# Last turns of a transformer kernel: low halves on VectorE, a pipelined softmax list, the last output product in one piece

## The reference

```
h = tokens(x)                                   # an S4D kernel, made once for all batches
h = h + attention(layernorm(h))                 # 32 query heads, 8 key heads, head size 32, causal, rotary
h = h + layernorm(h) @ W.T + b + sum_e alpha_e * lora_e(layernorm(h))   # 4 active experts of rank 8, alpha by a router
```

## Time and profile before

| what | us |
|---|---|
| median of 3 runs (2893.61 to 2898.27) | 2895.41 |
| the profiled execution: device time | 2895.14 |
| its span, first to last instruction | 2893.2 |
| TensorE busy | 2799.6 (97%) |
| VectorE busy | 2366.2 (82%) |
| ScalarE busy | 1918.2 (66%) |
| GpSimd busy | 1970.2 (68%) |
| mean granted TensorE clock, share of full | 0.991 |
| the ending, from TensorE's first scores of Z to the end of the span | 2811.05 to 2893.2 |

### The profile page before, as it was taken

How to read it: one execution, slowest core, us unless ns; L and a number is a source line. 1 busy time by engine, 2 the same in 40 slices (tenths; PEclk the granted TensorE clock), 3 DMA queues, 4 the chain that set the end, 5 groups by cost and what they waited for, 6 DMA issues and landing times.

```text
span 2893.2 us, 61884 instructions
## 1 busy us (share of the span) xinstructions
PE 2799.6 (97%) x16932; PEld 1408.5 (49%) x16932; DVE 2366.2 (82%) x8776; ACT 1918.2 (66%) x5986; POOL 1970.2 (68%) x1730
## 2 busy tenths in 40 slices
PE   6788899999999999999999999999999999999997
PEld 5665444444444444444444444444444444444443
DVE  9987788888888888888888888888888888888784
ACT  8887766666666666666666666666666666666662
POOL 4542677777777776777777777777767777777763
PEclk9999899999999999999999999999999999999999
DMA  7884677666666666666666666666666666666763
GB/s 246 231 217 135 142 153 150 149 149 151 151 143 152 146 156 147 151 149 147 152 148 149 149 150 151 143 152 147 156 149 148 150 146 152 150 149 149 152 132 78
DMA packets 1220851, 442.64 MB, mean 153 GB/s; under 512 B 1167120, under 2 KB 1175568, under 8 KB 1220640
## 3 DMA queue, kind: packets, MB, share of 16 engines
q1 hardware_dynamic: 1220640, 440.69, 66.7%
HBM read 88.22 MB, written 67.11 MB: 54 GB/s over the span
## 4 chain that ended last, share of the span: by engine, by line
PE 89%; DVE 3%; DMA 3%; ACT 2%; issue 1%; POOL 1%; SPq 1%; DVEq 0%; ACTq 0%; POOLq 0%
PE bank_b L2068 44%; PE bank_a L2068 22%; PE bank_c L2068 11%; PE score L2031 4%; PE kps L581 2%; PE pv L2057 2%; DMA tok_h<-kout 2%; PE bank_b L2057 1%; PE bank_b L2227 1%; DMA xc<-in_x_dram 1%; PE pv L2160 1%; ACT kout L358 1%; ACT probs L1440 0%; PE bank_c L2121 0%; PE pv L2121 0%
## 5 line engine op out<-in xcount | busy, mean ns | idle before, releaser
L1440 ACT ACTIVATE probs<-probs,negmax 128x128 f32<-128x128 f32 x2016 | 777.3, 387 | 247.4 <-DVE negmax L1658 247.3
L1303 POOL TENSOR_TENSOR p_hl<-probs,p_hl 128x512 f16<-128x512 f32 x503 | 607.6, 1208 | 333.9 <-ACT p_hl L1449 331.4
L1299 POOL TENSOR_TENSOR probs<-probs,rsum 128x512 f32<-128x512 f32 x503 | 547.6, 1089 | 183.5 <-DVE rsum L1669 183.1
L1658 DVE CUSTOM_DVE_ANT_0 probs<-score,table,scal 128x128 f32<-128x128 f32 x2016 | 589.0, 347 | 78.1 <-issue 77.4
L2068 PE MATMUL bank_a<-qkv_hi,xt 128*128 128x512 f16 x2048 | 642.6, 380 | 2.0 <-DMA xt<-xy_hl 2.0
L2068 PE MATMUL bank_b<-b_hi,yt 128*128 128x512 f16 x1952 | 610.7, 379 | 0.0
L1449 ACT ACTIVATE p_hl<-probs 128x512 f16<-128x512 f32 x503 | 314.5, 625 | 417.8 <-POOL probs L1299 417.8
L1712 DVE TENSOR_TENSOR heads<-rope_a,heads 128x512 f16<-128x512 f32 x319 | 388.1, 1232 | 30.0 <-ACT heads L1470 29.9
L2068 PE MATMUL bank_a<-qkv_lo,xt 128*128 128x512 f16 x1024 | 389.7, 381 | 0.0
L1440 ACT ACTIVATION_READ_ACCUMULATOR probs<-probs,negmax 128x1 f32 x2016 | 376.5, 187 | 0.0
L2068 PE MATMUL bank_b<-o_hi,at_hi 128*128 128x512 f16 x992 | 376.4, 379 | 0.0
(11 more groups left out here) (311 smaller groups left out, 4590.2 us busy)
## 6 DMA issues: line engine op xcount, KB each, us to landing
hin<-tok_h SPq DMA_DIRECT2D x64, 512.0 KB, 3.2
r<-tok_h SPq DMA_DIRECT2D x64, 512.0 KB, 3.8
out_dram<-r SPq DMA_DIRECT2D x63, 512.0 KB, 3.0
tok_h<-kout SPq DMA_DIRECT2D x60, 512.0 KB, 6.1
probs_t<-p_hl SPq DMA_TRANSPOSE x512, 3.1
xc<-in_x_dram SPq DMA_DIRECT2D x32, 128.0 KB, 4.5
raw_a<-in_L_attn_wq_dram SPq DMA_DIRECT2D x4, 1024.0 KB, 9.2
raw_b<-in_L_attn_wo_dram SPq DMA_DIRECT2D x8, 512.0 KB, 4.8
```

What stands on the lines that cost most here:

```text
L1299: TT(x, x, rsum[:, u % 4].unsqueeze(2).to_broadcast([P, GR, T]), ALU.mult).then_inc(s_norm, 1)
L1303: TT(p_hl[:, u % 2, 1], probs[:, u % 4], p_hl[:, u % 2, 0], ALU.subtract).then_inc(s_plo, 1)
L1440: ins = A(probs[:, u % 4, g], probs[:, u % 4, g], ACT.Exp, bias=negmax[:, u % 4, g:g + 1], scale=-1.0, accum_out=sums[:, u % 4, g:g + 1])
L1658: ins = V.tensor_tensor_reduce(probs[:, u % 4, g], score[u % 2][:, g], mask, col(U_SC), 3e38, ALU.add, ALU.min, negmax[:, u % 4, g:g + 1])
```

## The change

- GpSimd: the subtractions `low(X)` and `low(Y)` are gone, the bias additions of X and Y move behind all groups, `shift_of(X)` moves ahead of group 0 and `shift_of(Y)` between groups 6 and 7. The groups are pipelined: normalisation u, then the low half of u-1.
- VectorE: two new functions make whole rows and low rows for X, Y and Z. The list is reordered: X's second addition and statistics come first; the whole and low rows of Y stand around `routes(X)` and ahead of `weigh(X)`.
- ScalarE: `norm2` writes only the high half. `norm2(X)` moves up, `router_exp(X)` behind `probs_high(Z, 5)` but still ahead of `exps(7)`, `turned_z(X)` behind `probs_high(Z, 7)`.
- SyncE: the transpose of X's rows moves between groups 0 and 1, the last transpose of heads behind it.
- TensorE: `scores(7)` ahead of `ffn(X, 0)`; `attend(Z, 1)` ahead of `wo(Z)`; the four quarters of `wo(Z)` in a row, and `route(Y)` and `ffn(Y)` behind them.

```diff
@@ SyncE @@
                 residual(Y)
+                turn_probs(Z, 0)
+                turn_rows(X)
                 sp.wait_ge(s_hlo, Z * 5 + MADE[3])
                 sp.wait_ge(s_score, Z * 8)
                 sp.dma_start_transpose(stack[:, 3], heads[:, BLOCK[3]].rearrange("p h t -> p (h t)")).then_inc(s_st[3], 16)
-                turn_probs(Z, 0)
-                turn_probs(Z, 1)
-                turn_rows(X)
-                for u in range(2, 8):
+                for u in range(1, 8):
                     turn_probs(Z, u)
@@ GpSimd @@
                 def add_bias(c):
                     pool.wait_ge(s_yhi, c + 1)
-                    if c == Z:
-                        pool.wait_ge(s_ylo, c + 1)
+                    pool.wait_ge(s_ylo, c + 1)
...
                 normalise(Y, 7)
                 probs_low(Y, 7)
+                shift_of(X)
                 normalise(Z, 0)
+                for u in range(1, 7):
+                    normalise(Z, u)
+                    probs_low(Z, u - 1)
+                shift_of(Y)
+                normalise(Z, 7)
+                probs_low(Z, 6)
+                probs_low(Z, 7)
                 add_bias(X)
                 add_bias(Y)
@@ ScalarE @@
-                    ins = A(xy_hl[:, 0], r[:, c % 2], ACT.Identity, bias=shift2[:, 0:1], scale=rstd2[:, 0:1])
-                    if c != Z:
-                        ins = A(xyn[:, :], r[:, c % 2], ACT.Identity, bias=shift2[:, 0:1], scale=rstd2[:, 0:1])
-                    ins.then_inc(s_yhi, 1)
+                    A(xy_hl[:, 0], r[:, c % 2], ACT.Identity, bias=shift2[:, 0:1], scale=rstd2[:, 0:1]).then_inc(s_yhi, 1)
...
                 exps(0)
+                norm2(X)
                 exps(1)
...
                 exps(6)
+                probs_high(Z, 5)
                 router_exp(X)
-                probs_high(Z, 5)
                 exps(7)
                 probs_high(Z, 6)
-                turned_z(X)
                 norm2(Y)
                 probs_high(Z, 7)
+                turned_z(X)
@@ VectorE @@
+                def whole_rows(c):
+                    dve.wait_ge(s_rstd2, c * 2 + 2)
+                    if c == X:
+                        dve.wait_ge(s_xlo, CB)
+                    TS(xyn[:, :], r[:, c % 2], rstd2[:, 0:1], shift2[:, 0:1], ALU.mult, ALU.add).then_inc(s_xyn, 1)
+
+                def low_rows(c):
+                    dve.wait_ge(s_xyn, c - X + 1)
+                    dve.wait_ge(s_yhi, c + 1)
+                    TT(xy_hl[:, 1], xyn[:, :], xy_hl[:, 0], ALU.subtract).then_inc(s_ylo, 1)
...
                 invert(Y, 7)
+                add_wo(X, 1)
+                spread(X)
                 maxima(0)
                 attention_low(Y, 0)
                 maxima(1)
+                whole_rows(X)
                 invert(Z, 0)
+                maxima(2)
+                low_rows(X)
+                invert(Z, 1)
...
                 spread(Y)
-                routes(X)
                 maxima(7)
                 invert(Z, 6)
+                whole_rows(Y)
+                routes(X)
+                invert(Z, 7)
+                low_rows(Y)
                 weigh(X)
                 add_ffn(X, 0)
-                invert(Z, 7)
+                add_ffn(X, 1)
                 attention_low(Z, 0)
-                add_ffn(X, 1)
+                attention_low(Z, 1)
                 add_lora(X, 0)
                 add_lora(X, 1)
...
@@ TensorE @@
                 scores(6)
                 route(X)
-                ffn(X, 0, 0, 4)
                 scores(7)
-                ffn(X, 0, 4, 8)
+                ffn(X, 0, 0, 8)
                 ffn(X, 1, 0, 4)
                 turn_z(X)
                 ffn(X, 1, 4, 8)
                 pe.wait_ge(s_max, Z * 8 + 7)
                 attend(Z, 0)
                 lora(X)
+                pe.wait_ge(s_max, Z * 8 + 8)
+                attend(Z, 1)
                 wo(Z, 0, 0, 4)
                 wo(Z, 1, 0, 4)
-                pe.wait_ge(s_max, Z * 8 + 8)
-                attend(Z, 1)
-                route(Y)
-                ffn(Y, 0, 0, 3)
                 wo(Z, 0, 4, 8)
                 wo(Z, 1, 4, 8)
-                ffn(Y, 0, 3, 8)
+                route(Y)
+                ffn(Y, 0, 0, 8)
                 ffn(Y, 1, 0, 4)
                 turn_z(Y)
                 ffn(Y, 1, 4, 8)
```

More of the change, by code:

```diff
@@ L1382, in shift_of @@
                     TT(shift2[:, :], mean2[:, :], rstd2[:, :], ALU.mult).then_inc(s_rstd2, 1)
-                def low(c):
-                    pool.wait_ge(s_yhi, c + 1)
-                    TT(xy_hl[:, 1], xyn[:, :], xy_hl[:, 0], ALU.subtract).then_inc(s_ylo, 1)
                 def add_bias(c):
                     pool.wait_ge(s_yhi, c + 1)
-                    if c == Z:
-                        pool.wait_ge(s_ylo, c + 1)
+                    pool.wait_ge(s_ylo, c + 1)
                     TT(r[:, c % 2], r[:, c % 2], keep["bias"][:, :], ALU.add).then_inc(s_bias, 1)
@@ L1395, in ending @@
                 probs_low(Y, 7)
+                shift_of(X)
                 normalise(Z, 0)
-                probs_low(Z, 0)
-                normalise(Z, 1)
-                probs_low(Z, 1)
-                shift_of(X)
-                normalise(Z, 2)
-                low(X)
-                probs_low(Z, 2)
-                normalise(Z, 3)
-                probs_low(Z, 3)
-                add_bias(X)
-                normalise(Z, 4)
-                probs_low(Z, 4)
-                normalise(Z, 5)
-                probs_low(Z, 5)
-                shift_of(Y)
-                normalise(Z, 6)
-                probs_low(Z, 6)
-                normalise(Z, 7)
-                probs_low(Z, 7)
-                low(Y)
+                for u in range(1, 7):
[5 more added lines that the diff above has]
+                probs_low(Z, 7)
+                add_bias(X)
                 add_bias(Y)
@@ L1604, in ending @@
                 probs_high(Z, 1)
-                norm2(X)
                 attention_high(Y, 1)
@@ L1952, in ending @@
                    rope_a[:, 8:16].unsqueeze(2).to_broadcast([P, 8, 2, HD]), hi, ALU.subtract).then_inc(s_hlo, 1)
-                maxima(2)
-                invert(Z, 1)
-                add_wo(X, 1)
-                spread(X)
                 maxima(3)
+                attention_low(Y, 1)
                 invert(Z, 2)
-                attention_low(Y, 1)
                 maxima(4)
@@ L1968, in ending @@
                 spread(Y)
-                routes(X)
                 maxima(7)
                 invert(Z, 6)
+                whole_rows(Y)
+                routes(X)
+                invert(Z, 7)
+                low_rows(Y)
                 weigh(X)
                 add_ffn(X, 0)
-                invert(Z, 7)
+                add_ffn(X, 1)
                 attention_low(Z, 0)
-                add_ffn(X, 1)
+                attention_low(Z, 1)
                 add_lora(X, 0)
                 add_lora(X, 1)
-                attention_low(Z, 1)
-                routes(Y)
                 add_wo(Z, 0)
@@ L1983, in ending @@
                 spread(Z)
+                routes(Y)
+                whole_rows(Z)
                 weigh(Y)
-                dve.wait_ge(s_rstd2, Z * 2 + 2)
-                dve.wait_ge(s_ylo, Z)
-                TS(xyn[:, :], r[:, Z % 2], rstd2[:, 0:1], shift2[:, 0:1], ALU.mult, ALU.add).then_inc(s_xyn, 1)
-                dve.wait_ge(s_xyn, 1)
-                dve.wait_ge(s_yhi, Z + 1)
-                dve.wait_ge(s_yt, Z * 16)
-                TT(xy_hl[:, 1], xyn[:, :], xy_hl[:, 0], ALU.subtract).then_inc(s_ylo, 1)
+                low_rows(Z)
                 add_ffn(Y, 0)
```

## The result

| what | before | after |
|---|---|---|
| median of 7 runs, us | 2895.05 (2892.99 to 2898.27) | 2903.68 (2902.59 to 2907.06) |
| ratio, with its 95% interval | | 1.0033 (1.0024 to 1.0043) |
| the profiled execution: device time, us | 2895.14 | 2902.59 |
| its span | 2893.2 | 2900.6 |
| TensorE's first scores of Z, to the end of the span | 2811.05, 82.15 us | 2810.66, 89.94 us |

The kernel became slower by 0.33%, or 8.6 us between the medians. The forecast was 2900.6 us with a range up to 2904.5, so the time lies inside; but I had given "within 0.2%" the largest chance (0.50), and it is slower by more than that. Everything ahead of the ending is the same code, and the profile puts the loss where the forecast had put it, into the ending, 7.8 us.

A forecast was written before the change was run, and what follows sets the result against it. Batch Z's softmax chain, for which TensorE waits, was taken to bound the ending. turn_z(X) at 2851.9 plus 7.35 gave W = 2859.25; plus 39.2, a span of 2898.45; plus 2.2, 2900.6 us. Range 2893.5 to 2904.5.

The forecast's parts named there:

- within 0.2%: Whole kernel: time not told from no change, 2889.6 to 2901.2 us; chance 0.50, against slower 0.40 and faster 0.10.
- the queue: Rival, SyncE: rows of X and heads delay group 1's transpose, landing 2 us later at 2831.8; 2902.6 us, chance 0.24.
- W: Ending, first product of wo(Z,0) on TensorE: 2849.07 before, forecast 2859.25, ten us later, with 39.2 us to the end.
- part 3: Softmax list of batch Z: weigh(X) comes late, two bias additions add 2 x 2.2 us, turn_z(X) at 2851.9.
- e7: Start of the exponentials of group 7 on ScalarE: forecast 2840.7, before 2841.03; GpSimd's last low half ends 6.4 us later.
- the landing of group 1: SyncE's transpose of group 1: issued 2826.8, landed 2829.8; ScalarE's high half of group 3 needs that buffer.
- the base: Kernel before, last part of the ending: 25.9 us to ffn(Y,1)'s last product, then 18.2 us to the end.
- Part 1: Last output product in one piece on TensorE: 21.0 us instead of 25.9, 4.9 us saved, tail of 18.2 unchanged.
- Part 2: Start of the ending: wo(Y,0,4,8) at 2823.2 instead of 2826.07, 2.9 us for TensorE, worth nothing at the end.
- five us gained on GpSimd come to 0.3: Softmax list: router_exp(X) waits behind Y's scale and whole_rows(Y), so group 7's exponentials start at 2840.7 instead of 2841.03.
- faster rival: Softmax list: GpSimd sets the pace, group 5 ends at 2832.7; time 2888.6 us, or 2891.0 at lower clock; chance 0.10.
- The port: VectorE instructions with two SBUF inputs and GpSimd ones reading SBUF exclude each other; bias additions cost 2 x 2.2 us.

The follow-up runs named there:

- experiment 2: Changed kernel with GpSimd's two bias additions made to wait for the products of weigh(X); ratio to the kernel before 1.0017.
- experiment 1: Changed kernel with weigh(X) ahead of invert(Z,7) and low_rows(Y) on VectorE; 2895.91 us, ratio to the kernel before 1.0007.
- Experiment 3: Changed kernel with SyncE transposing the rows of X and the last heads ahead of group 0; ratio to the kernel before 1.0028.
- the second profile: The kernel before and the changed kernel each run once more with nothing edited; ratios 1.0001 and 1.0033.
- experiment 6: Kernel before with only GpSimd's list pipelined (next group normalised ahead of the last one's low half), low rows staying on GpSimd; 2890.69 us, ratio 0.9987.
- experiment 4: Kernel before with only TensorE's new order of the ending, scores(7) ahead of ffn(X,0) included; ratio 1.0013.
- 10: On experiment 6: wo(Z) in one piece ahead of route(Y) and ffn(Y), with attend(Z,1) behind its first quarter; 2887.66 us, ratio 0.9979 to the kernel before.
- experiment 8: On experiment 5: VectorE's first maxima back ahead of X's last addition, and its whole and low rows of X moved back; ratio to the kernel before 0.9981.
- experiment 5: On Experiment 3: weigh(X) and routes(X) earlier, Y's rows later; ScalarE and SyncE reordered; a quarter of wo(Z) ahead of attend(Z,1); 2888.0 us, 0.9978 to the kernel before.
- experiment 7: Kernel before with only the low rows of X and Y moved from GpSimd to VectorE, weigh(X) ahead of Y's; ratio 1.0000.

## Why the prediction was right, and where it was wrong

**The mechanism was right, the call was not.** From a change of 5.2 us (2900.6 for 2895.4) I had put "the same" first; it was 8.6 us. The time is inside the range only because the range reached out towards the queue, a rival. In the profile are `turn_z(X)` starved by 15.2 us (I had said 10 to 14), the last product of `weigh(X)` as its releaser, both bias additions between its products, the lower clock behind, no wait ahead of `route(Y)`, 39.2 us from W to the end (39.21 and 39.23 measured), `router_exp(X)` waiting for VectorE with group 7 behind it, and `low_rows(Y)` longer than 1.23 us (1.97). Removing the two additions gave back 4.46 us in experiment 2, for which part 3 writes 2 x 2.2 and adds 4.3; the whole place of `weigh(X)` was 10.2 us in experiment 1. From e7 on the steps are nearly exact: the last low half ended at e7 + 6.4 us, as forecast. Only the second addition came in elsewhere: it held the first product into `zs`, and not the last one, which waits for a semaphore.

**The step that failed is the landing of group 1, in part 3.** The sum had it issued at 2826.8, +15.75, and landed 3.0 us later, +18.75. It was issued at +15.93 and landed at +20.68, 4.7 us later. ScalarE's high half of group 3 and all behind it moved with it: e7 is at +31.52 where part 3 had +29.65, 1.9 us late, and `turn_z(X)` at +42.95 where it had +40.85. This is the rival "SyncE's queue", which had group 1 land at 2831.8 (+20.75) and the sign decided "from 0.6 us on". I gave it 0.24, and took for the forecast the median of ten transposes. The kernel before had a nearer neighbour: the rows of X, and 1.9 us behind them a group, landed in

```profile
yt<-xy_hl SPq DMA_TRANSPOSE x1, 4.7
probs_t<-p_hl SPq DMA_TRANSPOSE x1, 3.6
```

With 3.6 us in place of 3.0 the sum is 0.6 us longer, which is just where the sign turned. Experiment 3 corrects the rival too: the queue is 0.8 us of the 1.7, and the other 0.9 stay when it is empty; their cause stays open.

**A second weak term is the base.** Part 1 took 44.1 us from W to the end of the kernel before, and in it 1.7 us of low clock behind the wait for the rows of Y. Of the three profiles with this wait only the one shown has that; in the second profile, and in experiment 6 (2.28 us), it is 42.4. So the change was credited with 4.9 us, of which 1.7 were there in some executions only. The same holds for the 5.0 us for the twelve products behind `turn_z(X)`: right for the profile shown, too long for the second. Between the first two profiles, then, the base explains nothing, the endings differ by 7.8 us; between the second two they differ by 7.9, 88.33 less 80.44. The medians differ by 8.6 us, and by 10.0 in the second timing. What the rest is, two profiles of each kernel don't tell. The other low stretch, behind 5.43 us, also varies (5 us and some 2.6), but costs nothing: in the second profile TensorE waits 1.4 us longer for `turn_z(X)` and W is at +38.04 for +38.02.

**Part 1, the product in one piece,** is right in its size from W on and wrong in what it leaves out: it counted `attend(Z,1)` as saved and W as unmoved. Alone it makes the kernel slower (experiment 4, 1.0013), since TensorE idles 3.8 us in front of it. In the changed kernel the starved `turn_z(X)` hides this. One quarter further back the same idea gives 2.1 us (experiments 6 and 10).

**Part 2, the start,** gave 2.9 us for the second half of `wo(Y,0)`: it starts at +13.53 where it was at +15.02, 1.5 us earlier. The sum hadn't the wait of 2.06 us ahead of the third scores, nor the 3.2 us at the lower clock behind it. It was to be "worth nothing at the end", and experiment 8, in the order of experiment 5, bears that out.

**Part 3, the list: "five us gained on GpSimd come to 0.3".** In the changed kernel they come to less than nothing, 1.5 us later at e7 (of the sum for GpSimd's own pace, 2819.7 has no row, and with 6 x 2.15 it gives 2832.6, not 2832.7). The reason given, the scale of Y ahead of `routes(X)` ahead of group 7, is the right one: with those calls reordered e7 is 5.0 us earlier (experiment 5 beside 3). What I had not seen is that on the kernel before, the list alone is a real gain, 4.2 us at e7 and ratio 0.9987 (experiment 6). The "faster rival" had this mechanism and named the 0.74 us that GpSimd waited for ScalarE in each group; in the changed kernel the calls around it, and group 1's landing, kept it from coming true.

**The port.** The changed kernel bears out that the 128x1024 additions hold VectorE as the 128x512 forms do, 2.28 and 2.48 us for products of 0.2 to 0.3 us. The prediction priced it only for products with two SBUF inputs (operands in the core's on-chip memory), but the scalar product, with one tensor input, was held too: 0.93 us here and 1.06 us beside a normalisation in experiment 6, against 0.23 us in experiment 1. The same section of "SBUF — State Buffer" in the Trainium skill, "Who interferes with whom", says that `tensor_scalar` can enter a mode that takes both ports and then contends; the rows agree with it.

## What to carry to other kernels

When work moves to an engine whose order is written by hand, look at what stands behind it there: the moved work cost nothing by itself (experiment 7), while one small chain queued behind it, which TensorE waited for, came 10 us late and cost 0.26% of the time (experiment 1). A step that starves the bottleneck hides the price and the worth of every other part of the same change, so try the parts alone: of the three here one was a gain of 0.13%, one nothing, one a loss of 0.13% that turned into a gain when one call moved by twelve products (shown on top of the list, not alone). And a forecast near a bound should not lean on one profile's low-clock stretches, or on a median of transfers where one in nearly the same place is in the trace.

## What the runs showed of the hardware

- **Low clock behind short waits, and not each time.** The granted clock fell to the lower level behind waits of 2.06 us and of 3.3 us, in all profiles that have them. Behind the wait of 2.25 us it fell in one execution of the kernel before and not in the other, nor in experiment 6. Behind the wait of 15 us of the changed kernel the low stretch lasted 5.6 us in one execution and 2.7 in the other. What decides it, these runs don't show.
- **Transposes in a row mostly land late.** The rows of X, issued 1.3 us behind group 0, took 5.4 us to land, the heads behind them 4.6, group 1 behind these 4.7. In experiment 3, with nothing ahead of the rows, it was 3.6 and 3.1 us, and 3.9 for group 1, then 4.5 us behind the last transpose. What is ahead in the queue is not all of it: in the kernel before, the rows of X took 4.7 us with no transpose issued in the 5 us ahead of them.
- **Small VectorE products queue behind whole GpSimd instructions.** With several of them in a row and GpSimd's instructions queued as well, the two engines took turns: `za` (2.28 us, 0.19 in experiment 1) ended with the first addition, the first product into `zs` with the second (2.48 us for two, 0.29 in experiment 1).
